# Layer two's group turn in a new order: similarity first, output of one back behind the turns

## What is computed

```python
Sim = (enc @ w1)[:, :, None] + (dec @ w2)[:, None, :] + einsum('bid,bjd->bij', enc * w3, dec) + b_sim[0]
A = softmax(Sim, axis=2)
hq_hat = einsum('bij,bjd->bid', A, dec)
Batt = softmax(max(Sim, axis=2), axis=1)
hc_bar = einsum('bi,bid->bd', Batt, enc)[:, None, :]
feats = concatenate([enc, hq_hat, enc * hq_hat, enc * broadcast(hc_bar)], axis=-1)
hcq = feats @ W_qv + b_qv
```

## Time and profile before

| | |
|---|---|
| median of 3 runs | 1698.57 us (1696.36 to 1701.63) |
| the profiled execution | 1698.44 us |
| its span | 1696.6 us |
| TensorE busy | 1404.4 us, 83% |
| VectorE busy | 872.2 us, 51% |
| ScalarE busy | 553.5 us, 33% |
| POOL busy | 417.1 us, 25% |
| granted TensorE clock, mean | 0.883 |
| layer two's turns | 810 to 950 us of the span |

### The profile page before, as it was taken

The page is one execution under the profiler, slowest core; times in us unless marked ns, Lnnn a source line. Parts: engine busy times, 40 slices in busy tenths (PEclk is TensorE's granted clock), DMA queues, the critical chain, the costliest instruction groups (busy, mean ns, idle before and its releaser), DMA issues. The chain is left out here.

```text
span 1696.6 us, 26265 instructions
## 1 busy us (share of the span) xinstructions
PE 1404.4 (83%) x8869; PEld 885.2 (52%) x8869; DVE 872.2 (51%) x2507; ACT 553.5 (33%) x1291; POOL 417.1 (25%) x729
## 2 busy tenths in 40 slices
PE   4788886994798875886888599473999999999998
PEld 2566663552576763564787377352444444444443
DVE  4576645874564643342455343474445555555525
ACT  1456554651565651222444133141011011011001
POOL 2666711102755501000244322541000000000000
PEclk8699987995788987998667699796999999999999
DMA  6676750004667528500010111231122112202200
GB/s 163 196 161 150 165 120 1 1 1 114 146 162 152 153 36 350 220 0 19 13 32 18 36 53 50 56 114 70 72 93 106 66 41 106 75 32 105 78 28 13
DMA packets 134175, 151.38 MB, mean 89 GB/s; under 512 B 12150, under 2 KB 117942, under 8 KB 128806
## 3 DMA queue, kind: packets, MB, share of 16 engines
q1 hardware_dynamic: 127494, 142.28, 28.7%
q0 software_dynamic: 3296, 6.76, 1.3%
q10 hardware_dynamic: 3264, 0.79, 0.2%
HBM read 99.33 MB, written 49.48 MB: 88 GB/s over the span
## 5 line engine op out<-in xcount | busy, mean ns | idle before, releaser
L2694 DVE TENSOR_TENSOR l3f_weighted_T<-l3f_w_e,l3f_xnT 128x512 f32<-128x512 f32 x128 | 88.3, 691 | 129.6 <-PE psum L2445 115.1
L2445 PE MATMUL psum<-l3f_weighted_T,w_l3f_q 128*128 128x512 f32 x256 | 133.7, 604 | 16.4 <-DVE l3f_weighted_T L2694 14.6
L2445 PE MATMUL psum<-l3f_weighted_T,w_l3f_k 128*128 128x512 f32 x256 | 131.6, 596 | 0.0
L2445 PE MATMUL psum<-l3f_weighted_T,w_l3f_v 128*128 128x512 f32 x256 | 131.4, 595 | 0.0
L710 DVE TENSOR_REDUCE l1x_minus_max<-psum 128x4 f32<-128x512 f32 x128 | 86.0, 687 | 88.1 <-PE psum L373 87.2
L2454 PE MATMUL psum<-l3f_weighted_T,w_l3f_o 128*128 128x512 f32 x256 | 124.4, 624 | 1.7 <-DVE l3f_weighted_T L2694 1.7
L2694 DVE TENSOR_TENSOR l3f_weighted_T<-l3f_w_e,l3f_oT 128x512 f32<-128x512 f32 x128 | 88.4, 692 | 57.2 <-PE psum L2454 30.5
L710 DVE TENSOR_REDUCE l0x_minus_max<-psum 128x4 f32<-128x512 f32 x128 | 85.4, 686 | 57.2 <-PE psum L373 56.5
L531 ACT ACTIVATE l0x_probsT<-psum 128x512 f32<-128x512 f32 x128 | 73.9, 594 | 52.6 <-PE psum L386 43.7
L111 POOL TENSOR_TENSOR l3f_ln_rstd<-l3f_ln_mean_var,eps 128x4 f32<-128x4 f32 x8 | 1.9, 243 | 355.5 <-DVE l3f_ln_mean_var L104 355.5
L531 ACT ACTIVATE l1x_probsT<-psum 128x512 f32<-128x512 f32 x128 | 73.8, 594 | 40.4 <-PE psum L386 31.3
(11 more groups left out here) (486 smaller groups left out, 3004.1 us busy)
## 6 DMA issues: line engine op xcount, KB each, us to landing
l3f_w_e<-l3f_weights_scratch SPq DMA_DIRECT2D x32, 1024.0 KB, 4.6
sorted_x<-zeros SPq DMA_DIRECT2D x1, 16896.0 KB, 59.2
l0x_k_scratch<-l0x_k_parts SPq DMA_DIRECT2D x24, 384.0 KB, 4.0
l0x_k_stack<-l0x_k_scratch SPq DMA_DIRECT2D x16, 576.0 KB
l0x_q_stack<-l0x_q_scratch SPq DMA_DIRECT2D x48, 192.0 KB
l1x_k_scratch<-l1x_k_parts SPq DMA_DIRECT2D x24, 384.0 KB, 5.5
l1x_k_stack<-l1x_k_scratch SPq DMA_DIRECT2D x16, 576.0 KB
l1x_q_stack<-l1x_q_scratch SPq DMA_DIRECT2D x48, 192.0 KB
```

The source lines that it names most:

```text
L2445: ins = pe.matmul(bank[:, :], w[name][:, e, :], xe[:, e % 2, :], start=(e == 0), stop=(e == NE3 - 1))
L2694: dve.tensor_tensor(xe[:, e % 2, :], wE[:, g % 2, e, :], src, ALU.mult).then_inc(s_xe, 1)
```

## The change

It changes four places in `layer2`. A new semaphore `s_own` counts the one-column products. In `similarity` these products and their wait for h-bar go behind the 128x128 products, and each part signals by itself. TensorE's turn becomes: similarity, count of s-3, turn of h2 (s-2), turn of xn (s+1), turn of the row maximum, output of s-1, turn of the attention; the rest stays. VectorE's L1851 waits for `s_own` in addition, and its turn becomes: row_max, positions, stats1, normalise, token_max, update, token_total, stats2, token_probs_out; the rest stays. No instruction is added or taken away but the waits and the increment.

```diff
+        s_own = sem("own_sim_in_psum")
...
                 if g >= 1:
                     pe.wait_ge(s_p, g)
-                    pe.wait_ge(s_hb, g)
-                for c in range(GS):
-                    pe.matmul(bankM[:, c:c + 1], xnT[:, g % 3, seq(c)], w["l2x_w1"][:, :], start=True, stop=True)
                 for c in range(GS):
                     ins = pe.matmul(bankS[:, seq(c)], hwT[:, g % 2, seq(c)], k.ctxT[:, seq(g * GS + c)], start=True, stop=True)
                 ins.then_inc(s_s, 1)
+                if g >= 1:
+                    pe.wait_ge(s_hb, g)
+                for c in range(GS):
+                    ins = pe.matmul(bankM[:, c:c + 1], xnT[:, g % 3, seq(c)], w["l2x_w1"][:, :], start=True, stop=True)
+                ins.then_inc(s_own, 1)
...
                     similarity(s)
-                if 1 <= s <= NG:
-                    out(s - 1)
                 if 3 <= s < NG + 3:
                     count_before(s - 3)
-                if s < NG:
-                    turn_row_max(s)
                 if 2 <= s < NG + 2:
                     turn_h2(s - 2)
                 if s + 1 < NG:
                     turn_xn(s + 1)
+                if s < NG:
+                    turn_row_max(s)
+                if 1 <= s <= NG:
+                    out(s - 1)
                 if s < NG:
                     turn_attn(s)
...
                 dve.wait_ge(s_nmax, g + 1)
+                dve.wait_ge(s_own, g + 1)
                 dve.scalar_tensor_tensor(rmax[:, :], bankM[:, 0:GS], w["l2x_bsim"][:, 0:1], nmax[:, g % 2, :],
                                          ALU.add, ALU.subtract).then_inc(s_rmax, 1)
...
                     row_max(s)
+                if 3 <= s < NG + 3:
+                    positions(s - 3)
                 if s + 2 < NG:
                     stats1(s + 2)
-                if 3 <= s < NG + 3:
-                    positions(s - 3)
                 if s < NG:
+                    normalise(s)
                     token_max(s)
-                    normalise(s)
                 if 1 <= s <= NG:
                     update(s - 1)
+                if s < NG:
+                    token_total(s)
+                if 1 <= s <= NG:
                     stats2(s - 1)
                 if s < NG:
-                    token_total(s)
                     token_probs_out(s)
```

## The result

The changed kernel took 1678.86 us in the median of nine runs (1671.44 to 1695.0), the kernel before 1699.1 us in nine beside it; the ratio is 0.9889, with a 95% interval of 0.9859 to 0.992. That is faster by 1.1%, some 19 us (0.8 to 1.4%). The forecast was 1680 us.

A forecast was written before the change was run, and what follows sets the result against it. TensorE was taken as the bound, over half of each layer-two turn at half clock and idle while fast. Savings of 1.7 + 0.35 + 11.0 + 3.0 + 2.0 + 0.65 = 18.7 us from 1698.44 gave 1680 us, range 1664 to 1690.

The forecast's parts named there:

- First similarity: Layer two's first turn: similarity no longer waits behind the one-column products, 1.7 us saved outright.
- First turn: Layer two's first 12.75 us turn: row maximum 2.05 us earlier less 1.7 us of delays, 0.35 us net.
- the new wait: VectorE's own-similarity sum (L1851) waits for the one-column products, up to 1.0 us at the low clock.
- ScalarE's copies: First turn: copies for group 1 get ahead of the attention's copy, up to 0.7 us more delay.
- Filling turns: The two turns of about 15.1 us while the stage fills: 1.5 us saved each, 3.0 us.
- Four full turns: Layer two's four 16.09 us turns fall to 13.35 us, saving 2.74 us each, 11.0 us.
- The middle: Full turn taken as 13.35 us, between 12.6 and 14.2, as either half can hold the wait.
- Last turn and update: Stage's end: 2.0 us from the last turn's first part, 0.65 us from an earlier update.
- at no cost: Last turn: counts and the turn of two back lie in TensorE's gap before the output products, costing nothing.
- B: VectorE's new wait at L1851 delays normalising every turn; about 8 us gained, 1690.5 us, chance 0.12.
- C: TensorE's clock does not come up, turns need 19.4 us of work; +13 us, 1712 us, chance 0.06.
- A: TensorE's clock stays up and VectorE bounds at 10.6 us a turn; 34 us gained, 1664 us, chance 0.27.

The follow-up runs named there:

- Experiment 3: Changed kernel with VectorE's order put back to the one before, keeping its new wait; full turn 14.56 us, ratio 0.9951 to the kernel before.
- experiment 5: Changed kernel with the turn of xn (s+1) moved ahead of the turn of h2 (s-2); full turn 10.38 us, ratio 0.9767 to the kernel before.
- experiment 6: Changed kernel plus 8 spare identity transposes a turn behind the one-column products; full turn 11.41 us, ratio 0.9816 to the kernel before.
- 7: Changed kernel plus 4 spare identity transposes a turn behind the one-column products; full turn 10.47 us, ratio 0.9794 to the kernel before.

## Why the prediction was right

The total and the way to it held. That the median of 1678.86 us lies 1.1 from the forecast is partly luck, since nine runs span 24 us; the stage itself gained 17.0 us where the sum had 18.7. Term by term, in the profiled execution:

- *First similarity,* 1.7 us: 1.71 (row maximum 5.05 instead of 6.76 us behind the first turn of xn).
- *First turn,* 0.35 us: 1.00 (12.75 to 11.75). The delay by the new wait was 0.88 us of the up to 1.0 I named; of the further 0.7 us I gave to ScalarE's copies, 0.2 is left over.
- *Filling turns,* 3.0 us: 1.71 and 0.85, together 2.56.
- *Four full turns,* 11.0 us: 64.37 less 54.54, 9.83. The turn was 13.63 us where I took 13.35, within the 12.6 to 14.2. The middle was not well founded. Its lower end leaves the idle time out altogether; with 0.8 us of it in the low part the same working gives 6.9 + 5.6 + 0.8 = 13.3, so the two cases were 13.3 and 14.2. The run had the idle time in the fast part, and 0.60 us of it: 6.8 us, and 9.6 less 6.2 at the low clock, 6.8 more. Step by step: the high stretch kept its length (6.8 us), the work was the 9.7, the waits for the attention and the token total went. The idle time was 0.60 us, not 0.8, but at another place. I had it at L1527 behind VectorE's row sum; it lies at the turn of h two back, behind the second statistics that the change moves back, POOL's root and ScalarE. I had counted what the earlier token total gains and not what the later statistics cost. Experiment 3 bears this out: with the second statistics ahead of the token total again, TensorE's wait at L1564 is absent.
- *Last turn and update,* 2.65 us: 1.91 from the last row maximum to the first tile, but not by the parts I gave. Up to the weighing's end it took 10.8 us instead of 12.0, 1.2 less and not 2.0. The turn of h two back, which I put in the gap behind it "at no cost", waited 2.11 us for ScalarE's h, so the output products began 3.3 us behind the weighing and not 2.1. From their start to the update it took 4.8 us instead of 6.6, as the clock rose within them; that was luck of the clock. POOL's train of scatters moved with its start: 940.30 to 961.83 before is 21.5 us, 916.31 to 937.72 after is 21.4.

```profile
908.66 0.73 PE L1564 MATMUL psum<-constants,l_h_all 128*128 128x128 f32 x4 [2.11 <-ACT l_h_all L1674]
...
916.31 0.20 POOL L1785 TENSOR_TENSOR l_ln_rstd<-l_ln_mean_var,eps 128x4 f32<-128x4 f32 x1 [4.34 <-DVE l_ln_mean_var L1839]
...
937.72 0.44 PE L1626 MATMUL psum<-constants,l_x_tile 128*128 128x128 f32 x1 [11.26 <-DMA l_x_tile<-sorted_x]
```

*The rivals.* B (the new wait bounds) fell: 0.88 us in two turns, none later. The wait that the forecast named at the row maximum's turn (L1527, now L1530) did not come in the full turns. C (the clock does not come up) fell: it came up in every turn, in the output products. A had the right price, 10.6 us a turn and 1664 us, and did not happen, but it was much nearer than the prediction could know: experiment 5 reached it by moving one step (10.38 us, 1662.47 us). The prediction's reason against A, the fall with 5.30 of 6.90 us busy, was sound for the old idle time; with 6.21 of 6.80 the clock still fell, with 10.08 of 10.39 it held, and in experiment 6 it fell with 6.80 of 6.80.

The rule named there, that only long idle gaps let the clock fall (the Trainium skill, TensorE: Matmul & The Clock Gate, "HAM oscillation"), does not hold in these runs either: the longest gap in the changed kernel's full turns is 0.60 us, and experiment 6 saw a fall with none.

## What to carry to other kernels

In a stage whose TensorE clock rises and falls every turn, price a wait by what happens to the clock, and not by its length: look whether the granted clock falls in each turn, and which waits stand ahead of the fall. Then put steps whose data is long there (here the turn of xn) in front of steps whose data is just in time, and check the moved steps' own consumers on the other engines, since a step that is moved back on VectorE comes back as a wait two engines later. To judge such an edit, measure the stage between two marks in the trace, as the start of the same stage moved by up to 19 us from run to run.

## What the runs showed of the hardware that I had not expected

- Removing a wait of 0.60 us a turn shortened the turn by 3.25 us: 13.63 us at mean clock 0.75 with it, 10.38 at 1.00 without it. Experiments 5 and 7 show it by two different edits, one that moves work and one that adds some.
- More filling was not better: with 4, 8 and 12 spare transposes a turn the clock was low in part of none, two and one of the full turns. The falls behind this, at 883.5 and 897.2 with 8 and at 845.9 with 12 (from 840 on TensorE was busy for 6.00 of 6.00 us), came in stretches without idle time. Whether this is chance of timing was not tried.
- The gain of the parts does not add: 6.3 and 3.2 us of the stage for two parts alone, 17.0 for all, 33.5 with one step more moved (one execution each).
